# A graph-attention kernel: the sums of a sub-batch follow its scores by eleven steps instead of twelve, and in a step the attention weights are made before the sums

## What is computed

```python
Q = (jnp.einsum('nc,rch->rnh', x, Wq) + bq[:, None, :]).reshape(R, N, HEADS, OUT)   # K and V alike
score = jnp.sum(Q[edge_type, dst] * K[edge_type, src], axis=-1) * scale
seg = dst * R + edge_type                      # softmax over the edges of one node and relation
e = jnp.exp(score - segment_max(score, seg)[seg])
alpha = e / segment_sum(e, seg)[seg]
out = segment_sum(V[edge_type, src] * alpha[..., None], dst).reshape(N, HD) + bias
return _layernorm(x + out)
```

## Time and profile before

| what | value |
|---|---|
| time, median of 3 runs | 2515.57 us (2513.05 to 2515.9) |
| the profiled execution: its own time | 2516.02 us |
| its span in the trace | 2514.2 us |
| busy in the span: PE, DVE, ACT, POOL | 1600.0, 1718.9, 1192.3, 1628.7 us |
| edge loop, about | 785 to 2430 us of the span |

### The profile page before, as it was taken

The page is one execution under the profiler, slowest core; times in us unless marked ns, Lnnn a source line. Parts: engine busy times, 40 slices in busy tenths (PEclk is TensorE's granted clock), DMA queues, the critical chain, the costliest instruction groups (busy, mean ns, idle before and its releaser), DMA issues.

```text
span 2514.2 us, 26371 instructions
## 1 busy us (share of the span) xinstructions
PE 1600.0 (64%) x5873; PEld 1108.5 (44%) x5873; DVE 1718.9 (68%) x3712; ACT 1192.3 (47%) x4083; POOL 1628.7 (65%) x1745
## 2 busy tenths in 40 slices
PE   6999999999991354555555555555555455545546
PEld 2444544444440344444444444444444444444434
DVE  8888454443434777777777777777777777777758
ACT  2223111000001566666666666666666666666654
POOL 1000667777777777777777777777777777777504
PEclk9999999999995566665566566665665666666667
DMA  6333889999999766666666666666666666666406
GB/s 199 113 117 122 303 297 345 363 362 364 362 363 317 237 203 203 203 203 203 201 203 203 203 201 203 203 203 205 200 205 203 202 203 203 203 204 201 135 1 188
DMA packets 289040, 556.32 MB, mean 221 GB/s; under 512 B 44077, under 2 KB 171135, under 8 KB 288882
## 3 DMA queue, kind: packets, MB, share of 16 engines
q0 software_dynamic: 106496, 327.26, 43.1%
q1 hardware_dynamic: 146148, 159.43, 19.0%
q10 hardware_dynamic: 36238, 67.94, 7.6%
HBM read 399.62 MB, written 154.83 MB: 221 GB/s over the span
## 4 chain that ended last, share of the span: by engine, by line
POOL 33%; PE 26%; issue 16%; DVE 12%; ACT 7%; DMA 5%; SPq 1%; DVEq 0%; ACTq 0%; POOLq 0%
POOL region L405 22%; PE sums L566 21%; POOL region L410 11%; ACT region L800 6%; DVE region L881 5%; DMA region<-q_tab,qidx 3%; PE sums L627 2%; DVE region L1026 1%; DVE pairs L1024 1%; ACT pairs L789 1%; DVE acc L1087 1%; DVE region L1165 1%; PE sums L563 1%; DVE region L1168 1%; PE bank L587 0%
## 5 line engine op out<-in xcount | busy, mean ns | idle before, releaser
L627 PE MATMUL sums<-region 128*128 128x130 f32 x3328 | 775.0, 416 | 765.5 <-ACT region L800 745.7
L627 PEld LDWEIGHTS sums<-region 128*128 128x128 f32 x3328 | 704.9, 317 | 823.2 <-ACT region L800 818.1
L405 POOL DMA_INDIRECT region<-kv_tab,kvidx x832 | 790.9, 951 | 257.9 <-issue 245.0
L800 ACT ACTIVATE region<-region 128x64 f32<-128x64 f32 x3328 | 821.5, 333 | 0.0
L566 PE MATMUL sums<-region,acc 128*128 128x512 f32 (+2 forms) x1568 | 674.5, 577 | 1.0 <-DVE region L1003 0.8
L386 POOL DMA_INDIRECT region<-q_tab,qidx x400 | 381.1, 953 | 376.0 <-DMA q_tab<-region 253.2
L789 ACT COPY pairs<-region 128x1024 f32<-128x1024 f32 x208 | 211.2, 1015 | 696.4 <-DMA region<-q_pre 385.6
L1087 DVE TENSOR_TENSOR acc<-acc,sums 128x256 f32 x832 | 348.7, 419 | 271.1 <-PE sums L627 196.3
L410 POOL DMA_INDIRECT region<-q_tab,qidx x432 | 411.4, 952 | 131.6 <-issue 130.1
L566 PEld LDWEIGHTS sums<-region,acc 128*128 128x128 f32 (+1 forms) x1568 | 285.8, 190 | 302.2 <-issue 290.9
L1003 DVE TENSOR_TENSOR region<-sums,region 128x512 f32<-128x512 f32 (+1 forms) x245 | 168.9, 691 | 249.4 <-PE sums L566 249.1
(11 more groups left out here) (188 smaller groups left out, 813.2 us busy)
## 6 DMA issues: line engine op xcount, KB each, us to landing
kv_tab<-region ACTq DMA_DIRECT2D x48, 1280.0 KB, 7.5
q_pre<-region SPq DMA_DIRECT2D x400, 128.0 KB, 5.2
region<-q_pre SPq DMA_DIRECT2D x400, 128.0 KB, 3.5
q_tab<-region SPq DMA_DIRECT2D x48, 640.0 KB, 3.2
region<-q_tab,qidx POOLq DMA_INDIRECT x832, 3.8
region<-kv_tab,kvidx POOLq DMA_INDIRECT x832, 3.6
region<-in_x SPq DMA_DIRECT2D x96, 128.0 KB, 3.2
out<-region SPq DMA_DIRECT2D x48, 128.0 KB, 2.5
```

The costliest lines, as they stand in the source:

```text
L405: pool.indirect_dma_start(ring[:, s % KS, i, :], None, kv_tab, bass.IndirectOffsetOnAxis(ap=kvidx[:, t:t + 1], axis=0)).then_inc(s_got[s % ...
L627: done = nc.tensor.matmul(bank[i][:, h * W:(h + 1) * W], ring[:, q % KS, i, h * P:(h + 1) * P], oneh[:, q % 2, i, :], start=True, stop=True)
L800: done = nc.scalar.activation(ring[:, q % KS, i, h * D:(h + 1) * D], ring[:, q % KS, i, C + h * D:C + (h + 1) * D], ACT.Copy, scale=alT[:, ...
```

## The change

LAG goes from 12 to 11, so that in step s the sums are those of sub-batch q = s - 10. On PE `weights_a(s)` and `weights_b(s)` both stand ahead of the four tiles of `aggregate(q)`; on ACT both stand behind `lift(s)` and ahead of the four tiles of `payload(q)`. As chunk c's first sub-batch is 8c, its payload now falls into the same step 8c + 10 (phase 3) in which its weights are made. The numbers of instructions and the work of each stay the same.

```diff
-    LAG = 12
+    LAG = 11
...
                 q = s - LAG + 1
                 weights_a(s)
-                if 0 <= q < NSB:
-                    aggregate(q, (0, 1))
                 weights_b(s)
                 if 0 <= q < NSB:
-                    aggregate(q, (2, 3))
+                    aggregate(q, range(SB))
...
                 if s < NSB:
                     lift(s)
+                weights_a(s)
+                weights_b(s)
                 if 0 <= q < NSB:
-                    payload(q, (0, 1))
-                weights_a(s)
-                if 0 <= q < NSB:
-                    payload(q, (2, 3))
-                weights_b(s)
+                    payload(q, range(SB))
```

## The result

The changed kernel takes 2669.36 us (median of 4, 2665.1 to 2671.23) against 2515.74: a ratio of 1.0614, 95% interval 1.0601 to 1.0627. The forecast was slower, 2697 us, range 2600 to 2760. The profiled execution took 2669.65 us with a span of 2667.8; against 2516.02 that is +153.6 where +180.9 was forecast.

A forecast was written before the change was run, and what follows sets the result against it. POOL's gathers were taken to bound the kernel at 62.2 us a chunk. After the change, 35.56 + 10.83 + 11.03 + 12.04 = 69.46 us a chunk adds 180.9 us to 2516.02, giving 2696.9 us; range 2600 to 2760.

The forecast's parts named there:

- POOL sets the pace before, the lag alone is worth a payload at most: Edge loop: POOL's gathers take 62.2 us a chunk; LAG 11 alone saves only one payload at the end, 3.92 us.
- In four of eight steps payload, sums and weight work become one series; 69.46 us a chunk: Phases 1, 2, 3, 0: dependences run in series, 69.46 us a chunk against POOL's 62.2; chance 0.70.
- Phases 4 to 7: Payload starts after phase 3's payload: 4.92, 11.91, 16.83 and 23.82 us, two of the lifts waiting for scores behind sums.
- Phase 2's term: Payload to payload 11.03 us: 7.81 through the sums, then 3.22 of weight work, including 1.26 for row turns.
- Phase 1's term: Payload to payload 10.83 us: 7.81 through the sums, then 3.02 of weight work, including 0.66 to PE's turn back.
- Phase 0: Its payload starts 35.56 us after phase 3's, behind sums, the chunk's last scores, PE's turn and ACT's copy.
- The slack of 10.4 us: ACT's wait for gathered queries taken as slack a chunk, swallowing 10.4 of the 17.7 us added to the 51.8 us ring.
- POOL keeps up, with two us to spare: Tight at phase 0's lift: last gather lands at some 95.3 us, lift comes at 97.3; earlier ring slot worth nothing.
- The clock: Six sums a chunk on the path stay at the low clock, PE being idle at least 4 us ahead of each.
- POOL stays the bound: Rival: the series hides over 7.3 us a chunk more, so only the tail pays, +8.8 us, 2524.8; chance 0.08.
- full clock: Rival: all six sums on the path take 2.03 us, 58.6 us a chunk, under POOL's; 2519.4 us; chance 0.07.
- Faster: Rival: in the tail the weight work gets clear of the sums, -12.3 us, 2503.7; chance 0.03.

The follow-up runs named there:

- experiment 2: Kernel before with LAG 11 and the new order on PE and ACT in phase 3 alone: 2517.66 us, ratio 1.0012.
- experiment 11: Kernel before with LAG 11, PE's new order in every step, ACT's new order only in phase 3: 2511.95 us, ratio 0.9996.
- Experiment 6: Kernel before without the query gather of each sub-batch's fourth tile from the 13th sub-batch on: 2376.6 us.
- experiments 1: Changed kernel with LAG 12 instead of 11 and alT doubled: 2724.47 us, ratio to before 1.0831.
- 9: Changed kernel with LAG 12 and alT doubled, without the fourth tile's query gather from the 13th sub-batch on: 2664.13 us.
- 10: Changed kernel with 13 ring slots (KS) instead of 14: 2735.37 us.
- experiment 3: Changed kernel with PE and DVE at LAG 12, ACT as it was, so sums run one step behind the payload: 2511.40 us, ratio to before 0.9981.
- experiment 8: Changed kernel without the second product of all four tiles' sums: 2526.34 us.

## Why the prediction was right, step by step

- *POOL sets the pace before, the lag alone is worth a payload at most.* Right as a bound: experiment 2 is level with before, and the 3.92 us forecast for the end show neither there nor in experiment 11.
- *In four of eight steps payload, sums and weight work become one series; 69.46 us a chunk.* Right in mechanism, 1.18 too long. The starts of the payloads, mean of the 13 chunks between 1000 and 2400 us whose eight starts the timeline shows whole, step by step for phases 4, 5, 6, 7, 0, 1, 2, 3: 4.77, 7.14, 5.49, 6.32, 11.54, 10.52, 10.34, 12.16 us (over all 19 whole chunks of that window no mean differs from these by more than 0.06). Forecast were 4.92, 6.99, 4.92, 6.99, 11.74, 10.83, 11.03 and 12.04. Phases 4 to 7 agree in sum (23.72 and 23.82), not one by one: in phase 6 the lift waits 0.60 us for DVE's scores (1744.53), a wait that the forecast put at nothing. It drops out of the sum, because phase 7 is counted from the sums behind phase 5's payload.
- *Phase 2's term was mis-sized by 0.69 us.* I gave the row turns 1.26 us, two pairs of 0.63 at the low clock. They ran at the high level: 1714.85 to 1715.44, 0.59 [the PE rows above], with a granted clock of 1.00 in that stretch, after 0.50 during the 3.84 us of sums ahead of them (1709.67 to 1713.51).
- *Phase 1's term by 0.31 us.* The 0.66 from carries to PE's turn back came from a row in whose wait half a sum of the old order still stood (the 2.07 us of the earlier trace rows have a sibling from 2386.73 to 2388.67). In the new order nothing stands there: the carries end at 1705.23 and PE's turn back at 1705.56, 0.33. Phase 0 was 0.20 shorter. Together -1.18 x 25 = -29.5 us, which with +2.2 at the ends makes up 2696.9 against 2669.65.
- *The slack of 10.4 us swallows that much of 17.7.* The reading was wrong: not all of ACT's idle time ahead of the lift was slack that could be used. Experiment 6 found a period of 56.6, not 51.8. The sum didn't depend on it, since it set the series against POOL's 62.2, not against the slack.
- *POOL keeps up, with two us to spare.* Right for lag 11: ACT never waits for a gather. With lag 12 or 13 slots it doesn't (experiments 1, 9, 10). The margin was thin; I had written that the earlier slot is worth nothing, true in the old order and false in the new one, where it is worth 55 us.
- *The clock.* The six sums on the path at the low level: right for all but a few. Of 136 between 900 and 2450 us, 127 took over 3.8 us and nine 3.15 to 3.59. PE's idle time of at least 4 us ahead of each was forecast too high for two of them: it is 3.30 us ahead of phase 5's (1743.98) and under 2 ahead of phase 7's in four chunks, and the nine shorter sums are of these two phases. The one at 2.06 us (1749.45, phase 6), with a granted clock of 1.00, is none of the six; it starts 1.63 us after the sum before it has ended. The Trainium skill, TensorE: Matmul & The Clock Gate, Part 1, says that activity releases the halved clock; here the trace agrees: the high level came behind 3.83 us of sums, at 1749.45 and in the row turns at 1714.85, and the sum behind a gap of 4.38 us (1755.89) took 3.84 again. A short gap alone didn't bring it: the sum at 1736.84, 0.93 us behind another, took 3.83.
- *The rivals.* "POOL stays the bound" and "full clock" would have left POOL waiting for "issue" alone; it waits for sums. "Faster" had its point of decision at whether the sums of q - 1 are finished when the weights are asked for; in experiment 3, where they belong to an older payload, the last chunk's weights indeed come 3.9 us sooner after the last gather (29.1 us against 33.0).

## What to carry to other kernels

When two halves of a step run on different engines, moving one behind the other's whole work may add no instruction and still turn overlap into a series: write down, for each step, the chain from the start of a piece to the start of the same piece in the next step, and compare its sum over a period with what the bounding engine needs. An idle engine's wait ahead of one instruction is not yet slack: here 10.4 us a chunk were read and 5.6 could be used. And if an order has to change for one step of eight, change it in that step.

## What the runs showed of the hardware

- TensorE's granted clock was 0.50 over 1350 us of the loop in experiment 8, with PE busy for 438 of them, against 0.61 in the changed kernel with 726 of 1550. So the shorter sums came with the low clock for the transposes too: phase 2's row turns took 1.02 us (from 1700.89 us on) where they took 0.59.
- An addition of 128 x 256 values on VectorE that needs the result of the one before it took 0.42 us and started 0.20 after that one's end, in experiment 8 and, at 1739.67 to 1741.51 us, in the changed kernel. So 0.62 us a tile was the floor here, under PE's 0.96.
